# A local transformer's softmax: the exponentials of a step's second score bank read PSUM with the row maximum as bias

## The reference

```python
def local_attention(q, k, v):                 # 16 heads of 64, windows of 32 tokens
    bk2, bv2 = (look(bk), look(bv))           # each window sees itself and the one before: 64 keys
    ...
    sim = jnp.einsum('bhwie,bhwje->bhwij', bq, bk2) * QK_SCALE
    sim = jnp.where(mask, -jnp.finfo(sim.dtype).max, sim)
    attn = jax.nn.softmax(sim, -1)
    out = jnp.einsum('bhwij,bhwje->bhwie', attn, bv2)
...
for i in range(DEPTH):                        # DEPTH = 6
    x = attn_layer(shift_tokens(x), Wqkv[i], q_scale[i], k_scale[i], Wo[i]) + x
    x = ffn_layer(shift_tokens(x), ln_g[i], ln_b[i], W1[i], b1[i], W2[i], b2[i]) + x
```

## Time and profile before

| | |
|---|---|
| median of 3 runs | 2799.79 us (2796.5 to 2806.28) |
| the profiled execution | 2800.2 us |
| its span, first to last instruction | 2798.4 us |
| busy over the span: PE, DVE, ACT, POOL | 80%, 69%, 45%, 40% |
| mean granted TensorE clock | 0.893 of full speed |
| time of the 96 steps of the transformer | about 770 us to 2410 us of the span |

### The profile page before, as it was taken

How to read it: one execution, slowest core, us unless ns; L and a number is a source line. 1 busy time by engine, 2 the same in 40 slices (tenths; PEclk the granted TensorE clock), 3 DMA queues, 4 the chain that set the end, 5 groups by cost and what they waited for, 6 DMA issues and landing times. The chain is left out here.

```text
span 2798.4 us, 83518 instructions
## 1 busy us (share of the span) xinstructions
PE 2245.9 (80%) x36280; PEld 1553.3 (56%) x36376; DVE 1929.3 (69%) x4359; ACT 1271.8 (45%) x2309; POOL 1130.9 (40%) x834
## 2 busy tenths in 40 slices
PE   6834938644699999999999989999999999788182
PEld 3523824323366666666666666666666666554172
DVE  4461225576799888988898988888989898444311
ACT  2311303252356656554656555656565656233030
POOL 0004050000376565656555655665556565200304
PEclk9956968866799999999999999999999999789586
DMA  7102010000011121112111211121111111300022
GB/s 253 41 2 61 28 41 1 1 0 0 27 33 29 33 60 32 37 33 60 32 37 32 59 33 37 33 60 32 37 32 29 32 37 33 108 2 2 20 66 59
DMA packets 71859, 110.86 MB, mean 40 GB/s; under 512 B 11394, under 2 KB 56712, under 8 KB 64966
## 3 DMA queue, kind: packets, MB, share of 16 engines
q1 hardware_dynamic: 67398, 97.88, 12.6%
q0 software_dynamic: 4096, 7.63, 0.9%
HBM read 42.29 MB, written 16.78 MB: 21 GB/s over the span
## 5 line engine op out<-in xcount | busy, mean ns | idle before, releaser
L2583 POOL TENSOR_TENSOR mem<-mem 128x512 f32<-128x512 f32 x384 | 572.6, 1498 | 606.7 <-DVE mem L2142 589.7
L1865 PE MATMUL ps<-mem 128*128 128x512 f32 x768 | 396.2, 620 | 3.8 <-DVE mem L2142 1.3
L2422 ACT ACTIVATE mem<-ps 128x512 f32<-128x512 f32 x384 | 219.6, 601 | 226.6 <-PE ps L1886 226.1
L2401 ACT ACTIVATE mem<-ps 128x512 f32<-128x512 f32 x384 | 228.7, 600 | 162.6 <-PE ps L1865 121.7
L2137 DVE TENSOR_TENSOR mem<-ps,mem 128x512 f32<-128x512 f32 x384 | 258.7, 674 | 22.5 <-ACT mem L2401 22.4
L2142 DVE TENSOR_TENSOR mem<-ps,mem 128x512 f32<-128x512 f32 x384 | 260.9, 679 | 0.0
L1886 PEld LDWEIGHTS ps<-mem 128*128 128x128 f32 x1536 | 186.4, 144 | 122.7 <-issue 104.3
L1947 PEld LDWEIGHTS ps<-mem 64*64 64x64 f32 x12288 | 193.3, 136 | 79.4 <-issue 77.2
L1874 PE MATMUL ps<-mem 128*128 128x512 f32 x384 | 207.2, 623 | 31.5 <-ACT mem L2461 19.2
L2149 DVE TENSOR_REDUCE mem<-mem 128x16 f32<-128x1024 f32 x192 | 231.8, 1207 | 0.0
L2596 POOL TENSOR_TENSOR mem<-mem 128x1024 f32<-128x1024 f32 x96 | 182.3, 1899 | 100.6 <-DVE mem L2211 100.6
(11 more groups left out here) (281 smaller groups left out, 4129.2 us busy)
## 6 DMA issues: line engine op xcount, KB each, us to landing
mem<-mem SPq DMA_DIRECT2D x48, 768.0 KB, 5.8
mem<-in_Wqkv SPq DMA_DIRECT2D x6, 1536.0 KB, 6.9
mem<-mem SPq DMA_DIRECT2D x36, 256.0 KB, 3.5
x<-mem SPq DMA_DIRECT2D x10, 512.0 KB, 6.5
mem<-x SPq DMA_DIRECT2D x16, 320.0 KB, 5.6
y<-mem SPq DMA_DIRECT2D x16, 320.0 KB, 2.5
mem<-in_W12T SPq DMA_DIRECT2D x8, 512.0 KB, 7.3
mem<-in_L3W SPq DMA_DIRECT2D x16, 256.0 KB, 5.1
```

The costliest lines, as they stand in the source:

```text
L1865: e.matmul(self.K.ps[:, o, :], self.columns(u, bb), self.K.l2[l % 2]["Wqkv"][:, 512 * i:512 * i + 512], start=True, stop=True, skip_group_ ...
L2401: e.activation(self.SQ[:, 512 * j:512 * j + 512], self.K.ps[:, self.ROTATE[i], :], ACT.Square).then_inc(s("squared"), 1)
L2422: e.activation(to, view(self.K.ps[:, self.FEATURE[i], :], "p (c q) -> p c q", c=4), ACT.Copy).then_inc(s("placed"), 1)
L2583: e.tensor_tensor(t1[:, cols], t1[:, cols], self.T2[:, cols], ALU.add).then_inc(s("rotated"), 1)
```

## The change

The subtraction of the second half (`odd = 1`) goes away on DVE. DVE's maximum of that half is written with the sign turned (`negate=True`) and is what signals `lessened`. On ACT the one exponential over 1,024 columns becomes one over the 512 columns of the first half in SBUF, which can begin once the first half is there, and eight over 64 columns each, which read the second half's scores in PSUM, bank 2, and take the negated maximum of their 64 keys as bias, one word per partition. Bank 2 is then free when the last of these is done (event `exped`, now counted twice a step), not when DVE has subtracted. `v_normalise` waits for the second count.

```diff
         for odd in range(2):
-            self.freed[banks[odd]] = [s.at("lessened", 2 * g + odd + 1)]
+            self.freed[banks[odd]] = [s.at(("lessened", "exped")[odd], 2 * g + odd + 1)]
...
+        if odd:
+            if g >= 2:
+                e.wait_ge(*s.at("exped", 2 * g - 2))
+            e.tensor_reduce(m, sc, AX.X, ALU.max, negate=True).then_inc(s("lessened"), 1)
+            self.fill()
+            return
         t = v(e.tensor_reduce(m, sc, AX.X, ALU.max))
         self.fill()
         e.wait_ge(v.sem, t)
-        if g >= 2 and odd == 0:
+        if g >= 2:
             e.wait_ge(*s.at("p_turned", 2 * g - 2))
...
     def v_normalise(self, e, g):
-        e.wait_ge(*s.at("exped", g + 1))
+        e.wait_ge(*s.at("exped", 2 * g + 2))
...
     def a_exp(self, e, g):
-        p = view(self.PB[g % 2], "p o c w j -> p (o c w j)")
-        e.wait_ge(*self.s.at("lessened", 2 * g + 2))
-        e.activation(p, p, ACT.Exp).then_inc(self.s("exped"), 1)
+        s, r = self.s, g % 2
+        p = view(self.PB[r][:, 0], "p c w j -> p (c w j)")
+        e.wait_ge(*s.at("lessened", 2 * g + 1))
+        e.activation(p, p, ACT.Exp).then_inc(s("exped"), 1)
+        e.wait_ge(*s.at("lessened", 2 * g + 2))
+        if g >= 2:
+            e.wait_ge(*s.at("p_turned", 2 * g - 2))
+        p = view(self.PB[r][:, 1], "p c w j -> p (c w) j")
+        for i in range(8):
+            last = e.activation(p[:, i], self.K.ps[:, self.SCORES[1], 64 * i:64 * i + 64], ACT.Exp,
+                                bias=self.mxs[r][:, 8 + i:9 + i])
+        last.then_inc(s("exped"), 1)
```

More of the change, by code:

```diff
@@ L1653 @@
                   rotated_half=4 * NG, rotated=4 * NG, square_sums=2 * NG, q_unit=NG, k_unit=NG, by_feature=4 * NG,
-                  placed=4 * NG, padded=NU, scored=2 * NG, lessened=2 * NG, exped=NG, inverses=NG, soft=NG, p_turned=2 * NG,
+                  placed=4 * NG, padded=NU, scored=2 * NG, lessened=2 * NG, exped=2 * NG, inverses=NG, soft=NG, p_turned=2 * NG,
                   p_cols=NG, p_cols_too=NG, values_mm=4 * NU, values=4 * NU, values_shifted=16 * (2 * NU - NF),
```

## The result

The changed kernel takes 2846.28 us in the median (2843.01 to 2853.03, 4 runs) against 2803.03 for the kernel before on the same chip: a ratio of 1.0157, with a 95% interval of 1.0133 to 1.0181. It is slower by some 43 us; forecast were 60, with 20 to 95 as the range. The profiled execution took 2843.01 us, its span is 2841.2 us, 42.8 more than before.

A forecast was written before the change was run, and what follows sets the result against it. PE was taken to set the pace, DVE close behind. Waits of 77 us in plain steps, 1 in step 0 and 8 at layer starts, less 26 given back, made +60: 2860 us, range 2820 to 2895.

The forecast's parts named there:

- The place: Bank 2 before rotate 2: PE would wait 0.99 us at 78 places for ACT's last small exponential.
- step 0: The step without weigh: PE's wait there would add 1 us.
- The price of the nine instructions: On ACT: the first half's exponential takes 0.53 us of the queue, the eight small ones 1.82 us.
- The sum of the waits: PE before rotate 2 in plain steps: 78 places of 0.99 us, 77 us.
- The layer starts: Four layer starts, where longer exponentials lie on the path to values 1: 2.0 us each, 8 us.
- What it gives back: PE's waits for POOL and for DVE's first subtraction shrink or go: 26 us together.
- each shrinks by at most 1.6: Seven POOL waits of 2.7 us behind the softmax lose at most 1.6 us each, 11 us.
- the faster rival: Small exponentials 0.09 us or less apart, PE doesn't wait, some 17 us gained, 2783 us; chance 0.06.
- The emptying after the exponentials: ACT's emptying, 1.3 us later, costs PE 0 at values 1 and projection; 14 us if uncovered.
- the swallowed one: Wait at rotate 2 only 0.2 us a place, 2799 us, no difference; chance 0.05 within 0.3%, 0.04 swallowed in part.
- TensorE's clock: Clock falls after PE's waits would add to the loss; given little, 0.12 together with dear small ones, above 2890 us.
- Theory B: Set up for the follow-up runs: the loss is ACT's extra work as such, 96 us, delaying whatever stands behind it.

The follow-up runs named there:

- experiment 4: Changed kernel with the two score banks exchanged in even steps, so the small exponentials read bank 3 there: 2803.85 us, ratio 1.0020 to the kernel before.
- Experiment 3: Changed kernel with the first half's exponential moved ahead of the square of rotate 1 on ACT: 2814.94 us, ratio 1.0061 to the kernel before.
- Experiment 1: Changed kernel with one 512-column or four 128-column exponentials for the eight, constant bias, second half's scores left out: 2782.53 us with one, 2801.85 us with four.
- Experiment 2: Banks 2 and 5 exchanged for rotate 2 and 3 (not at w = 5): changed kernel 2820.77 us, kernel before as control 2809.95 us.
- experiment 6: Both bank exchanges and early first half, w = 1 in the old form: 2790.89 us; change in even steps alone, score banks exchanged there: 2785.47 us.
- the kernel with four: Changed kernel with four exponentials of 128 columns in place of eight of 64, constant bias, scale zero: 2801.85 us, ratio 1.0014 to the kernel before.

## Why the prediction was right, and where it was off

*The place.* PE waits for bank 2 before rotate 2: shown by the timeline, and by experiment 4, which takes the wait away in even steps and leaves ACT's work as it is. Experiment 3 shortens it by an order alone. Experiment 1 takes it away too, but with it ACT's extra work. 82 waits stand in the profile against 83 forecast (78, the four layer starts and step 0). At w = 5 the "up" product hides it from step 13 on, as forecast; step 37 after the change:

```profile
1421.77 1.13 PE L2013 MATMUL ps<-mem 128*128 128x512 f32 x2
1422.74 1.07 PE L1865 MATMUL ps<-mem 128*128 128x512 f32 x2
```

*The price of the nine instructions.* Forecast 0.53 and 1.82 us, measured 0.52 and 1.74. The distance worked out from four short instructions without bias and four long ones with it, 0.214, was 0.20. By the rule of the Trainium skill, page "ScalarE: Activation LUTs", section "What ACT_TABLE_LOAD costs", an estimate of the distance would have been 0.240 us, and of one alone 0.333; the trace agrees with the second (0.336) and not with the distance, since these records overlap by 0.14 us and not by 0.093.

*The sum of the waits.* Forecast 77 us in plain steps. The 90.3 us less step 0 (3.2 us) and less the four layer starts are 60 us, or 0.78 a place where I had 0.99. Three things make the difference. The chain was 0.08 us shorter. In 17 steps, 16 of them even, the wait shown is only 0.3 to 0.7. And a wait of 0.84 as shown stands for 0.92 between starts (2.81 - 1.89), since the records overlap otherwise. Step 0 was put at 1 us, and that was right: its wait is 3.2 us, but from its score mask to rotate 2 it takes 6.92 us where it took 5.87, since before the change rotate 0 and 1 ran slower there (3.48 us for what now takes 1.98) and rotate 2 waited 0.5.

*The layer starts.* Forecast 8 us for the four. Step 17 after the change, answering to the earlier trace rows:

```profile
1054.86 2.08 PE L1865 MATMUL ps<-mem 128*128 128x512 f32 x2 [6.25 <-ACT mem L2459]
1056.73 1.91 PE L1874 MATMUL ps<-mem 128*128 128x512 f32 x2
```

Rotate 2 now stands behind the exponentials, at half clock (granted 0.50), and values 1 behind it. The four waits (6.25, 6.91, 6.67 and 7.13 us) are 27.0 us against 19.2. From ACT's instruction that the DMA releases to values 1 there were 3.06 us in each of the four, and now there are 5.65: 2.6 more, 10 us in all. Both terms of the forecast (1.3, and 1.4 if rotate 2 must come after) were paid, where 2.0 had been taken between them.

*What it gives back.* Forecast 26 us; the two waits named shrank by 9.9 and 7.8, together 18. The step that was too rich is "each shrinks by at most 1.6": the 14 short waits for POOL went, but the seven long ones (w = 1) fell only from 2.74 to 2.08, by 0.66. The 1.6 were 0.99 for PE arriving later and 0.60 for DVE being earlier, and the timelines show what became of either. These times, in us from the start of weigh at w = 1, are the same in all seven places within 0.02:

| | before | changed | one exponential (experiment 1) |
|---|---|---|---|
| rotate 2 starts | 2.0 | 2.9 | 2.0 |
| ACT's guess of the feed-forward's root done | 4.5 | 4.2 | 3.9 |
| DVE starts the sum of the exponentials | 8.95 | 8.64 | 8.33 |
| PE has done what stands before the transposes (L1992) | 9.75 | 10.10 | 9.18 |
| POOL done, the transposes start | 12.49 | 12.17 | 11.87 |

PE is 0.91 us late at rotate 2, but only 0.35 at the transposes: half way it used to wait for DVE's normalised rows, and doesn't any more. (An even step begins with the transposes of the probabilities, ahead of the scores.) At the turn from step 41 to 42, this is the second half of L1992 before the change, and the transposes with the change:

```profile
1477.49 0.66 PE L1992 MATMUL ps<-mem 128*128 128x128 f32 x4 [0.34 <-DVE mem L2255]
1497.04 1.09 PE L1924 MATMUL ps<-mem 128*128 128x128 f32 x8 [2.08 <-POOL mem L2612]
```

And DVE is only 0.31 us earlier at the sum of the exponentials, where it could be 0.62, as the run with one exponential shows. It waits there for ACT's guess (L2446, `a_mlp_guess`), which stands behind the exponentials and the emptying, while before the change ACT waited for DVE at this point:

```profile
DVE mem L2159 <- ACT mem L2446: 5.5, 11, 1.0
```

With 0.35 and 0.31 in place of 0.99 and 0.60 the 0.66 come out. The wait for DVE's rows that went (2.4 us in seven places) is a gain that the forecast didn't count. With one exponential, what DVE's lighter queue is worth measures 15 us, near the 17 of the faster rival, but not by that rival's sum: the long waits stay at 2.69 where they were to lose 0.6 each, since PE arrives 0.57 earlier too. That the totals are so near is in part luck.

*The sum.* PE's waits grew by 50 us, the span by 42.8. Between the first and the last score mask the changed execution is 44.8 us longer: PE stands still 51.3 us more, and its busy time is 6.6 us less (1546.6 to 1540.0). About half of that lies in the transposes L1924, of which fewer ran at half clock: of the seven groups after a wait of 2.74 us four took 1.96 or 1.97 us, of those after 2.08 us none, six of them 1.09. The remaining 2 us lie outside, 1.3 of them ahead of the first mask, where nothing of the program is changed.

*The emptying after the exponentials*, taken at 0 with 14 us if its cover were gone: in the changed kernel values 1 waits for it once, 0.4 us. Experiment 2 took the cover away, and the wait was there: 0.3 us in most places, as forecast, and 1.05 at the four layer starts, but in 25 places and not in 46, 10.0 us in all.

*The rivals.* The faster one (small ones at 0.09 us) and the swallowed one fell with the measured 0.20. TensorE's clock did not fall after waits of 0.8 us: over 770 to 2455 us it is 0.98, as before, and the pair of matmuls after the wait takes 1.13 us. Theory B fell with experiments 3 and 4, and in experiment 6 the small ones run in 48 steps at no loss. What ACT's lateness does cost shows at two places: the 10.0 us of experiment 2, and the guess above.

## What to carry to other kernels

When an instruction is moved from one engine to another, look less at both engines' sums than at the buffer that it releases: find who writes it next, count back from there to the last thing that the new reader must wait for, and compare the two distances. Eight instructions of 64 columns cost ACT 1.74 us where one of 512 costs 0.68, and here most of the loss lay in 0.9 us of that distance. The cure was to give the late reader the buffer that is wanted last (score banks exchanged in even steps), and to keep the old form where no such buffer is to be had; and to look for what the new place of the buffer uncovers, since the first exchange, of banks 2 and 5, brought two other waits and uncovered a third.

## What the runs showed of the hardware

ACT instructions with a bias operand overlap more when they are short. Of 64 columns, 0.336 us alone, they come 0.20 apart (overlap 0.14). Of 128, in the kernel with four:

```profile
1423.29 1.14 ACT L2460 ACTIVATE mem<-ps,mem 128x128 f32<-128x128 f32 x4
```

With 0.375 us alone that is (1.14 - 0.375)/3 = 0.255 apart (overlap 0.12). Of 512 columns, on 77 partitions, 0.68 alone, they come 0.577 apart (overlap 0.10). The three distances lie on one line, an estimate from these three alone: some 0.15 us an instruction and 0.84 ns a column.

The length of a wait did not by itself settle the clock behind it. Before the change, after the same wait of 2.74 us, the eight transposes took 1.96 us at a granted clock of 0.51 in step 42 and 1.09 us at 1.00 in step 26.
